# Two norm applications in front of a grouped-query projection, moved from VectorE to ScalarE

## The reference, cut to what matters

```python
z = _layernorm(x)                      # (x - mean) / sqrt(var + eps)
h = rmsnorm(z, ln_w)                   # z * rsqrt(mean(z*z) + eps) * ln_w
q = (h @ wq).reshape(B, S, 16, 128)    # 2048 columns
k = (h @ wk).reshape(B, S, 4, 128)     # 512 columns
v = (h @ wv).reshape(B, S, 4, 128)     # 512 columns
q = apply_rope(q, cos, sin)
k = apply_rope(k, cos, sin)
...
x = o @ wo + z                         # z is also the residual
```

## Time and profile before

| | before |
|---|---|
| median of 3 runs (lowest, highest) | 2371.01 us (2369.51, 2371.94) |
| profiled execution: time | 2371.03 us |
| profiled execution: span | 2369.3 us |
| busy over the span: PE, DVE, ACT, POOL | 1930.7, 1630.7, 1084.4, 817.1 us |
| V matmuls of batch 0 begin | 1151.81 us from the span's start |
| QK matmuls of batches 0, 1, 2, 3 begin | 1160.18, 1205.70, 1252.35, 1297.89 us |
| last addition of the stage ends | 1329.73 us |

### The profile page before, as it was taken

How to read it: one execution, slowest core, us unless ns; L and a number is a source line. 1 busy time by engine, 2 the same in 40 slices (tenths; PEclk the granted TensorE clock), 3 DMA queues, 4 the chain that set the end, 5 groups by cost and what they waited for, 6 DMA issues and landing times. The chain is left out here.

```text
span 2369.3 us, 41415 instructions
## 1 busy us (share of the span) xinstructions
PE 1930.7 (81%) x12514; PEld 1511.7 (64%) x12514; DVE 1630.7 (69%) x3462; ACT 1084.4 (46%) x2414; POOL 817.1 (34%) x841
## 2 busy tenths in 40 slices
PE   5799853999999468997588699999989329999980
PEld 2455452999999243334466477777778329999980
DVE  5567367888888758883786577777744428888855
ACT  1166512444444115883101177777742027777740
POOL 2134222555555310001364677777700330000005
PEclk9789866999999688998798899999989559999995
DMA  3323000000000051220344423232272355555523
GB/s 131 127 71 84 23 1 28 26 27 18 27 27 0 24 188 52 71 56 6 107 124 115 133 90 111 89 111 90 92 255 84 119 201 202 203 201 220 221 80 100
DMA packets 101394, 232.97 MB, mean 98 GB/s; under 512 B 14840, under 2 KB 40824, under 8 KB 96192
## 3 DMA queue, kind: packets, MB, share of 16 engines
q1 hardware_dynamic: 94784, 218.85, 27.1%
q0 software_dynamic: 3072, 8.39, 1.1%
q10 hardware_dynamic: 3456, 4.72, 0.7%
HBM read 157.73 MB, written 72.88 MB: 97 GB/s over the span
## 5 line engine op out<-in xcount | busy, mean ns | idle before, releaser
L557 POOL TENSOR_SCALAR d_att_probs<-d_att_probs,d_att_rinv 128x128 f32<-128x128 f32 (+3 forms) x256 | 276.3, 1085 | 115.2 <-DVE d_att_rinv L568 114.8
L1432 DVE SCALAR_TENSOR_TENSOR b_acc<-bank,b_gates,b_acc 128x256 f32<-128x256 f32 x512 | 212.4, 477 | 41.7 <-PE bank L1347 41.7
L1400 POOL TENSOR_TENSOR b_moe_act_low<-b_moe_act,b_moe_act_high 128x512 fp32r<-128x512 f32 x136 | 175.8, 1293 | 177.6 <-ACT b_moe_act_high L1377 177.6
L455 PE MATMUL wide<-d_att_k,d_att_q 128*128 128x128 f32 (+3 forms) x512 | 182.3, 438 | 15.9 <-DMA d_att_k<-k_dram 15.9
L2015 PE MATMUL wide<-e_moe_hT_high,e_moe_w_high 128*128 128x256 f32 x644 | 183.1, 284 | 11.7 <-DVE e_moe_w_low L2085 11.7
L508 ACT ACTIVATE d_att_probs<-wide,d_att_nmax 128x128 f32<-128x128 f32 (+3 forms) x256 | 136.4, 533 | 111.8 <-DVE d_att_nmax L563 111.8
L2015 PE MATMUL wide<-e_moe_hT_low,e_moe_w_high 128*128 128x256 f32 x644 | 183.0, 284 | 0.0
L2015 PE MATMUL wide<-e_moe_hT_high,e_moe_w_low 128*128 128x256 f32 x644 | 183.0, 284 | 0.0
L910 DVE TENSOR_REDUCE c_att_rmax<-wide 128x2 f32<-128x1024 f32 x128 | 152.5, 1219 | 22.5 <-PE wide L687 21.8
L2148 POOL DMA_INDIRECT e_out_got<-y_slots,e_pos x32 | 31.3, 979 | 392.2 <-PEq L2142 383.0
L2085 DVE TENSOR_TENSOR e_moe_w_low<-e_moe_w,e_moe_w_high 128x768 fp32r<-128x768 f32 x161 | 151.2, 954 | 19.8 <-ACT e_moe_w_high L2045 17.2
(11 more groups left out here) (359 smaller groups left out, 6019.1 us busy)
## 6 DMA issues: line engine op xcount, KB each, us to landing
e_moe_w<-in_e_w SPq DMA_DIRECT2D x23, 2688.0 KB, 9.8
q_dram<-d_in_rot SPq DMA_DIRECT2D x64, 256.0 KB, 3.6
d_att_q<-q_dram SPq DMA_DIRECT2D x16, 1024.0 KB, 5.0
o_dram<-d_att_o SPq DMA_DIRECT2D x64, 256.0 KB, 2.0
d_out_oT<-o_dram SPq DMA_DIRECT2D x32, 512.0 KB, 5.5
b_moe_w<-in_b_w SPq DMA_DIRECT2D x17, 512.0 KB, 3.5
e_moe_h<-h_slots SPq DMA_DIRECT2D x23, 256.0 KB
y_slots<-e_moe_y SPq DMA_DIRECT2D x23, 256.0 KB, 9.7
```

Of the source, the lines that this page charges most:

```text
L455: nc.tensor.matmul(stile[qt], qs[s][:, u, qt * P:(qt + 1) * P], ks[s][:, 0, 0:w], start=True, stop=False)
L557: g.tensor_scalar(tile, tile, rinv[:, j, qt:qt + 1], None, ALU.mult).then_inc(scaled, 1)
L1400: g.tensor_tensor(ap[1][:, u % 4, :], act[:, u % 4, :], ap[0][:, u % 4, :], ALU.subtract).then_inc(act_low, 1)
L1432: nc.vector.scalar_tensor_tensor(out=tile, in0=y, scalar=gate, in1=tile, op0=ALU.mult, op1=ALU.add).then_inc(acc_done, 1)
```

## The change

Both applies go to ScalarE. As (x - mean) * r is x * r + (-mean * r), VectorE now makes `shift` = -mean * r, a 128x4 operation, after pair 1 (`shift_x`); ScalarE's new `keep_z` waits for it and does the four applies as `Identity` activations with scale `r` and bias `shift`. VectorE's `measure_z` (the statistics of z) waits for them and stands after pair 4. GpSimd's root for z moves from behind addition 3 to behind addition 5. ScalarE's new `keep_h` waits for that root and applies it as `Copy` activations with a scale. On ScalarE both stand between the copies of V and `keep_hT(b + 1)`; in the prologue in front of the high parts of the weights.

```diff
--- before.py
+++ after.py
@@ -1509,6 +1509,7 @@
         col, rope = sb("col", [P, KT]), sb("rope", [P, 2, 3, S])
         h = sb("h", [P, NQ, D])
         hT = [sb(f"hT_{part}", [P, KT, S], F32R) for part in ("high", "low")]
+        shift = sb("shift", [P, NQ])
         first, second = sb("first", [P, 2, 2, S]), sb("second", [P, 2, 2, S])
         rot = sb("rot", [P, NC, S])
 
@@ -1516,7 +1517,7 @@
         raw_v = rot[:, 10:12, :]
         CW = NC * P // 2
         halves = [slice(i * CW, (i + 1) * CW) for i in range(2)]
-        w_high, w_low, hT_high = sem("w_high"), sem("w_low"), sem("hT_high")
+        w_high, w_low, hT_high, shift_ready = sem("w_high"), sem("w_low"), sem("hT_high"), sem("shift_ready")
         qk_in, rope_in = [sem("qk_in0"), sem("qk_in1")], sem("rope_in")
         w_in, z_ready, h_ready, tr_done, hT_ready, v_done, v_kept, qk_done, terms, rot_ready, spare = (
             sem(n) for n in ("w_in", "z_ready", "h_ready", "tr_done", "hT_ready", "v_done", "v_kept", "qk_done",
@@ -1551,18 +1552,14 @@
 
             @block.vector
             def _(v):
-                def keep_z(b):
+                def shift_x(b):
                     norm_x.wait(v, b)
-                    for q in range(NQ):
-                        norm_x.apply(q, tile_of(z, b, q), tile_of(c.x, b, q)).then_inc(z_ready, 1)
+                    nc.vector.scalar_tensor_tensor(out=shift[:, :], in0=norm_x.mv[:, :, 0], scalar=-1.0, in1=norm_x.r[:, :],
+                                                   op0=ALU.mult, op1=ALU.mult).then_inc(shift_ready, 1)
+
+                def measure_z(b):
                     v.wait_ge(z_ready, b * NQ + NQ)
                     norm_z.statistics(v, b, lambda q: tile_of(z, b, q), rms=True)
-
-                def keep_h(b):
-                    norm_z.wait(v, b)
-                    v.wait_ge(tr_done, b * KT + KT)
-                    for q in range(NQ):
-                        norm_z.apply(q, h[:, q, :], tile_of(z, b, q), rms=True).then_inc(h_ready, 1)
 
                 def group(b, last):
 
@@ -1576,10 +1573,10 @@
                             v.wait_ge(qk_done, b * NC + (cc + 1))
                             nc.vector.tensor_tensor(out[:, p % 2, :, :], ps[cc % 4][:, :].unsqueeze(1).to_broadcast([P, 2, S]),
                                                     rope[:, kind, lo:lo + 2, :], ALU.mult).then_inc(terms, 1)
-                        if p == 2 and not last:
-                            keep_z(b + 1)
-                        if p == 6 and not last:
-                            keep_h(b + 1)
+                        if p == 1 and not last:
+                            shift_x(b + 1)
+                        if p == 4 and not last:
+                            measure_z(b + 1)
                     if not last:
                         low_hT(b + 1)
 
@@ -1590,8 +1587,8 @@
                                                        op0=ALU.mult, op1=ALU.subtract).then_inc(hT_ready, 1)
 
                 norm_x.statistics(v, 0, lambda q: tile_of(c.x, 0, q))
-                keep_z(0)
-                keep_h(0)
+                shift_x(0)
+                measure_z(0)
                 v.wait_ge(w_high, 1)
                 nc.vector.tensor_tensor(wv[1][:, :, :], raw_v, wv[0][:, :, :], ALU.subtract).then_inc(w_low, 1)
                 low_hT(0)
@@ -1613,7 +1610,7 @@
                         g.tensor_tensor(rot[:, 2 * p:2 * p + 2, :], first[:, p % 2, :, :], second[:, p % 2, :, :], ALU.add).then_inc(rot_ready, 1)
                         if p == 0 and not last:
                             norm_x.root(g, b + 1)
-                        if p == 3 and not last:
+                        if p == 5 and not last:
                             norm_z.root(g, b + 1, rms=True)
 
                 norm_x.root(g, 0)
@@ -1626,6 +1623,20 @@
 
             @block.scalar
             def _(s):
+                def keep_z(b):
+                    s.wait_ge(shift_ready, b + 1)
+                    hold(s, spare)
+                    for q in range(NQ):
+                        nc.scalar.activation(tile_of(z, b, q), tile_of(c.x, b, q), ACT.Identity, bias=shift[:, q:q + 1],
+                                             scale=norm_x.r[:, q:q + 1]).then_inc(z_ready, 1)
+
+                def keep_h(b):
+                    s.wait_ge(tr_done, b * KT + KT)
+                    norm_z.wait(s, b)
+                    hold(s, spare)
+                    for q in range(NQ):
+                        nc.scalar.activation(h[:, q, :], tile_of(z, b, q), ACT.Copy, scale=norm_z.r[:, q:q + 1]).then_inc(h_ready, 1)
+
                 def keep_hT(b):
                     for k in range(KT):
 
@@ -1639,8 +1650,12 @@
                         nc.scalar.copy(vals[:, bass.ds(b * KVH, KVH), q, :],
                                        pv[q % 2][:, :].rearrange("p (g d) -> p g d", d=GD)).then_inc(v_kept, 1)
                     if not last:
+                        keep_z(b + 1)
+                        keep_h(b + 1)
                         keep_hT(b + 1)
 
+                keep_z(0)
+                keep_h(0)
                 s.wait_ge(w_in, 32)
                 nc.scalar.copy(wv[0][:, :, :], raw_v).then_inc(w_high, 1)
                 keep_hT(0)
```

## The result

| | before | after |
|---|---|---|
| first comparison, median (lowest, highest) | 2371.94 (2369.51, 2372.32), 5 runs | 2354.73 us (2352.51, 2364.93), 5 runs |
| ratio of times | | 0.9942, 95% interval 0.9917 to 0.9966 |
| repeat, median | 2369.49, 15 runs | 2356.03 us (2350.66, 2363.80), 7 runs |
| its ratio | | 0.9942, 0.9919 to 0.9965 |
| profiled execution, span | 2369.3 | 2363.2 us |

Faster, by 13.8 us (8.1 to 19.7); that is the ratio's figure and the difference of the means, while the two medians lie 17.2 us apart. The profiled execution of after was the slowest of its five, so its span is not compared with a median; stages are compared instead. Each number of the last four lines is a distance between starts in TensorE's timeline, like the one that follows.

The account below looks back on a forecast made before the run. TensorE in `grouped_projection` was taken to wait for VectorE to empty PSUM banks. Three passes gaining 5.8 us of QK and 0.3 of handoff, minus 2.0 of prologue, gave 16.3 us off 2371.0: 2355 us, range 2348 to 2364.

Parts of the forecast that it names:

- A: Grouped projection: shift unhindered, QK chunks 28.0 us a pass, prologue 2.0 us later, 16.3 us gained, 2355 us; 50%.
- B: Loop: shift loses its turn to GpSimd's addition 1, TensorE stalls 1.3 to 1.8 us before chunk 14; 2362 us, 30%.
- the shift's price: VectorE's 128x4 `shift_x` after pair 1 in the loop: 0.2 us, taken as unhindered by GpSimd's addition.
- the wait of 0.8 us for the root: VectorE after chunk 3 in each pass: a new 0.8 us wait for GpSimd's root before the shift.
- the lost 5.8 us of QK: QK chunks take 33.8 us a pass but want 28.0; mostly a 3 us TensorE stall and slow matmuls behind it.
- ScalarE's prices: Moved applies on ScalarE: four `Identity` for z 1.9 us, four `Copy` for h 1.6 us, hidden in the loop.
- D: Loop: GpSimd's additions hold ScalarE's applies as they held VectorE's, making the kernel slower, about 2377 us; 4%.
- h ready in time: End of a loop pass: the last h apply is done at 25.3 us, before TensorE wants it at 28.0.
- Prologue 2.0 later: Batch 0, where nothing covers the applies: V matmuls start 2.0 us later, bounds 1.2 and 3.5.
- handoff 4.2 instead of 4.49: Transposes to V matmuls between batches: 4.2 us instead of 4.49, with GpSimd the near limit.
- C: Handoff falls to 2.8 us and the clock may stay up, V matmuls taking 5.6 us; 2347 us, 12%.
- I change nothing here and carry +-1.1 a pass: V matmuls after the handoff: times of 7.25 and 8.37 us left unchanged, with 1.1 us a pass either way.

Follow-up runs that it names:

- repeat: The changed kernel, with no further edit, run again and profiled a second time: median 2356.03 us in 7 runs, ratio 0.9942 to before.
- the kernel whose stage is 4.7 us shorter: Against the changed kernel, GpSimd starts addition 1 only when VectorE has made the shift: 2357.76 us, ratio 0.9951 to before.
- the best kernel: Changed kernel plus addition 1 waiting for the shift, z root behind addition 4, earlier `wv_high` cast, `wv_low` waiting for that root: 2345.69 us, ratio 0.9900.

## Why the prediction was right or wrong

**The time was foretold, its mechanism was not.** 2355 was the time of A; the median was 2354.73. But B is what happened, and B was priced at 2361 to 2364. In the stage A's sum wants 16.3 us and B's 7.3 to 10.3; measured are 9.97. The time lands on A's number by luck, by what other stages did in those executions. The repeat's profile shows it: 2354.79 us with the shift held in every pass, 9.9 us of it from this stage and another 6.3 us from the rest of the kernel, whose code is the same. In all fourteen profiles this rest took 2171 to 2184 us. The profiled execution of after alone would have said 2363 to 2365, and the kernel whose stage is 4.7 us shorter had a median of 2357.76, 1.7 us above the repeat's beside it. The medians of this comparison don't tell A from B; the stage does.

**The failed step** is the shift's price: "The shift comes at least 0.03 behind, so the nearest row says unhindered, but narrowly." It came 0.07 behind and was held for 2.35 us. The row of 1348.18 in the earlier trace rows, one case of an operation that began together with GpSimd's, was taken as the nearest. But GpSimd seems to have paid there. Its timeline:

```profile
1348.16 1.42 POOL L557 TENSOR_SCALAR d_att_probs<-d_att_probs,d_att_rinv 128x256 f32<-128x256 f32 x1
```

This is the 1424 ns of the earlier trace rows; the other 63 operations of that line and shape take 0.92 us. So the row reads as VectorE winning the turn, though its record begins 0.02 us after GpSimd's, and no case of the two going unhindered side by side. It was no evidence for an operation that loses. The 2.43 us row was misread too, as "the whole addition": it ran from 387.85 to 390.28 and the addition ended at 389.73, so it was held to that end and then took its own 0.55.

B's weight was wrong too: GpSimd's addition follows its own root, and the shift waits for that same root, so the two start together in every pass, by the order of the code and not by chance. B had 30%, and this was reason to give it the larger part.

The Trainium skill ("SBUF — State Buffer", Who interferes with whom) gave the right rule, that whichever of a VectorE instruction with two SBUF inputs and a GpSimd instruction that reads SBUF issues first holds the pair for all of it. The trace agrees: 2.35 us against 0.17. The row of 1361.48 does not bear out "for all of it", and it is one of fifteen alike in the profile of before: begun 0.14 to 0.27 us behind GpSimd's 1.56 us operation, VectorE's took 0.96 to 1.09 us instead of 0.69 and each time ended 0.33 us before GpSimd's did. It was held, but not to the end.

**B's own numbers** held: foretold chunk 4 at 9.9 to 10.2 us and measured 10.1; a stall of 1.3 to 1.8 before chunk 14, measured 1.37 to 1.40; handoff 4.7, measured 4.63 to 4.64; 3.1 to 4.1 us gained a pass, measured 11.2 / 3 = 3.7.

**Right:** the wait of 0.8 us for the root (0.80 to 0.81). The causes of the lost 5.8 us of QK: with the holding taken away QK is 28.0 us, to the tenth what was worked out from ten unhindered chunks. ScalarE's prices: 1.9 and 1.6 us, measured 2.08 and 1.71; not held by GpSimd, so D is out; no table load. The casts that were to speak against D did not: of their 0.61 us GpSimd was busy for 0.11 in 15 cases and for none in the sixteenth, so they did not run beside a busy GpSimd. What rules D out are the `Copy` of this kernel and the `Identity` of the kernel in which addition 1 waits. h ready in time: its applies are over at 1233.95 + 1.71 = 1235.66, 2.1 us before the transposes. Prologue 2.0 later, measured 2.24. The Trainium skill ("ScalarE: Activation LUTs", Rules for kernel authors) prefers VectorE for such work. The trace agrees for the prologue alone, where four z applies took 1.38 us on VectorE and 2.08 on ScalarE, four h applies 1.14 and 1.71; in the loop the runs speak against it: with the h applies back on VectorE the stage takes 187.23 us instead of 180.27.

**Mis-sized:** "handoff 4.2 instead of 4.49". It is 4.64 with the shift held and still 4.56 without. Two small causes were left out, as the timelines have it; no run takes them away one by one. L108 has two SBUF inputs as well and lasts 0.61 to 0.64 us instead of 0.16 beside GpSimd. And VectorE waits in front of chunk 16 until GpSimd's row of work from addition 5 has come to addition 6: taking the root out of that row gives 0.74 us.

**C, the short handoff with the clock up,** was right, but for another kernel: h alone on ScalarE gave just that, 2.82 and 5.70 us, where 2.8 and 5.6 were worked out. In the change as made the handoff is too long for it. The z root behind addition 5 is one part of that; without it and with the shift free the handoff is still 3.8 us, a microsecond above C's, and the clock stays up all the same. My working treated the V matmuls as "I change nothing here and carry +-1.1 a pass", though C's own estimate put 6 us on them. In the runs they are the largest single term after QK: 22.87 us for three batches before and after, 17.1 in the best kernel.

**How the best kernel's 24.2 us come about**, from the same starts: QK 3 x 5.79 = 17.4, V matmuls of batches 1 to 3 5.8, handoffs 3 x 0.69 = 2.1, batch 0's V 0.7, less 1.6 in the prologue: with the second decimals kept, 24.25.

**Open:** what decides the clock between 2.81 and 2.84 us of idle time, and why the V matmuls take 7.2 in one batch (granted clock 0.76) and 8.4 in the next (0.64) at equal idle time. Why the attention stage starts at a lower clock behind some of the kernels (0.52 to 0.69 against 0.78) wasn't tried. The length of the stage in front alone does not decide it: behind 177.03 us it was 0.52, behind 176.88 0.78.

## What to carry to other kernels

When work leaves one engine, look at which small operation is now made to start in the same instant as another engine's long one. If both are let go by the end of the same instruction and VectorE's has two SBUF inputs while GpSimd's reads SBUF, price the short one at the whole length of the other, and give the short one its turn with one wait on the long one's engine: here 0.34 us of GpSimd a pass bought 4.7 us of the stage. Look behind each handoff at what the matmuls do that follow it; 0.74 us less handoff went with 3.0 us a pass, and 0.8 us of work put in its way took the whole of it back. Where stages without a change differ by up to 5 us between executions, and everything outside the changed stage by 13, judge by the length of the changed stage, and by the whole time only what is larger than that.

## What the hardware showed that was not expected

- The holding works in both directions and on tiny operations. VectorE's 128x4 operation took 2.34 to 2.36 us beside GpSimd's addition, which had begun 0.05 to 0.07 us before it, and this in all 18 loop passes of the six executions that have the change's shift and no wait of addition 1 (0.16 to 0.17 in the prologue and with the wait). GpSimd's 128x4 root took 1.92 us instead of 1.01 beside VectorE's 1.22 us subtraction, begun 0.16 us before it.
- The hold did not go by whose record begins first when it was a near tie: at 0.02 us VectorE ran unhindered (one case, 1348.18) and GpSimd's operation took 1.42 instead of 0.92 us, at 0.05 to 0.07 us GpSimd ran unhindered, 18 times of 18.
- ScalarE was not held by GpSimd: four applies took 2.08 and 1.71 us beside its additions as without them.
- TensorE's clock after a handoff turns on little. The same 24 matmuls took 5.69 to 5.71 us behind 1.78 to 1.79 us (three of three) and 2.77 to 2.81 us (nine of nine) of idle time, and 7.1 to 8.5 us behind 2.84 us and more (in every handoff of the other kernels). The idle time in front is not all: batch 0's took 7.2 to 8.4 us behind 1.56 to 2.19 us, where the prologue had given TensorE only eight transposes and the granted clock stood at 0.50 when they began.
- A stage with the same code, the first attention, took 184.4 to 189.9 us in the fourteen profiles of this case, at three levels: nine stand within 184.4 to 184.8, two at 186.8 to 186.9, three at 189.8 to 189.9.
